# Part of the early loads and fills on ACT's queue, the first chunks also delivered turned, the first mixture's choices made for two or three chunks at a time, more tile buffers, and a new written-out order

## The reference, cut to what matters

```python
x = x + 0.5 * _L0_ffn_ref(_layernorm(x), ...)   # first mixture: 8 experts, 128 -> 512 -> 128, gelu
x = x + _L0_attn_ref(_layernorm(x), ...)        # conv, cumulative means of q and k, 128 -> 512 -> 128
x = x + 0.5 * _L0_ffn_ref(_layernorm(x), ...)   # first mixture again, same weights
x = x + 0.5 * _L1_ffn_ref(_layernorm(x), ...)   # second mixture: 16 experts, at most 320 tokens each
x = x + _L1_attn_ref(_layernorm(x), ...)        # a recurrence along each sequence
x = x + 0.5 * _L1_ffn_ref(_layernorm(x), ...)   # second mixture again

def _L0_ffn_ref(x, wr, br, w1, b1, w2, b2):     # of the 8 results only the chosen expert's is kept
    scores = einsum('bsh,he->bse', x, wr) + br
    expert_id = argmax(scores, axis=-1)
    h = gelu(einsum('bsh,ehf->ebsf', x, w1) + b1)
    y = einsum('ebsf,efh->ebsh', h, w2) + b2
    return einsum('ebsh,bse->bsh', y, one_hot(expert_id, 8))
```

## Time and profile before

| what | value |
|---|---|
| median of 3 runs | 824.54 us (823.46, 824.54, 829.46) |
| the profiled execution | 821.34 us, span 820.0 us |
| PE busy | 622.5 us, 76% |
| DVE busy | 444.1 us, 54% |
| POOL busy | 391.9 us, 48% |
| ACT busy | 336.5 us, 41% |
| mean granted clock of TensorE | 0.889 |
| moved by DMA | 94.87 MB, mean 116 GB/s |
| chain that ended last | PE 55%, issue 11%, DVE 10%, DMA 7%, POOL 6%, another core or an unknown queue 5% |

### The profile page before, as it was taken

How to read it: one execution, slowest core, us unless ns; L and a number is a source line. 1 busy time by engine, 2 the same in 40 slices (tenths; PEclk the granted TensorE clock), 3 DMA queues, 4 the chain that set the end, 5 groups by cost and what they waited for, 6 DMA issues and landing times.

```text
span 820.0 us, 13494 instructions
## 1 busy us (share of the span) xinstructions
PE 622.5 (76%) x3648; PEld 500.6 (61%) x3648; DVE 444.1 (54%) x1751; ACT 336.5 (41%) x993; POOL 391.9 (48%) x395
## 2 busy tenths in 40 slices
PE   6447588999988988996798742699965775397976
PEld 5437477978755755786688742476643664165654
DVE  5742145675889598563247633254436887043433
ACT  2113146646657535533347642343315543312411
POOL 1654535435421147245536667055464577234355
PEclk9998599999989999998899975699996975598998
DMA  8456278676200002344456323344533121233210
GB/s 323 142 188 202 86 214 257 173 217 217 79 1 0 1 21 94 96 128 134 121 163 195 99 70 145 82 140 117 155 97 103 56 68 63 73 104 98 62 31 13
DMA packets 74826, 94.87 MB, mean 116 GB/s; under 512 B 12610, under 2 KB 51305, under 8 KB 74496
## 3 DMA queue, kind: packets, MB, share of 16 engines
q1 hardware_dynamic: 64640, 79.46, 32.6%
q0 software_dynamic: 10112, 14.55, 5.3%
HBM read 65.71 MB, written 33.64 MB: 121 GB/s over the span
## 4 chain that ended last, share of the span: by engine, by line
PE 55%; issue 11%; DVE 10%; DMA 7%; POOL 6%; another core or an unknown queue 5%; ACT 3%; SPq 2%; DVEq 0%; ACTq 0%; POOLq 0%
PE ps L674 9%; PE ps L601 9%; PE ps L609 8%; PE ps L681 8%; POOL xs L1199 4%; PE ps L623 3%; PE ps L559 3%; PE ps L528 3%; PE ps L656 2%; PE ps L649 2%; DMA KC<-in_consts 2%; PE ps L664 2%; PE ps L592 2%; DMA xi<-xs 1%
## 5 line engine op out<-in xcount | busy, mean ns | idle before, releaser
L1108 ACT ACTIVATE ht<-ps,CL 128x128 f32<-128x128 f32 x368 | 103.8, 372 | 134.1 <-PE ps L601 77.9
L1199 POOL DMA_INDIRECT xs<-X,IDX x128 | 127.2, 994 | 63.1 <-issue 39.0
L1203 POOL DMA_INDIRECT y<-yt,xi x92 | 91.0, 989 | 124.2 <-DVE yt L909 104.5
L601 PE MATMUL ps<-xt,w1s 128*128 128x128 f32 x736 | 106.8, 295 | 24.6 <-DVE xt L903 12.6
L601 PEld LDWEIGHTS ps<-xt,w1s 128*128 128x128 f32 x736 | 97.0, 206 | 31.8 <-DVE xt L903 17.2
L609 PE MATMUL ps<-W,ht 128*128 x736 | 106.6, 296 | 10.4 <-issue 5.5
L609 PEld LDWEIGHTS ps<-W,ht 128*128 128x128 f32 x736 | 97.4, 208 | 16.6 <-issue 16.2
L1196 POOL TENSOR_TENSOR sma<-sma,MH 128x4 f32<-128x4 f32 (+1 forms) x40 | 48.4, 1215 | 64.5 <-DVE sma L719 53.4
L1165 ACT ACTIVATE hb<-ps 128x320 f32<-128x320 f32 x64 | 27.8, 437 | 108.0 <-PE ps L674 90.8
L1203 POOL DMA_INDIRECT y<-xu,x x36 | 34.3, 952 | 49.1 <-DVE xu L1017 33.9
L909 DVE SCALAR_TENSOR_TENSOR yt<-ps,xb 128x128 f32<-128x128 f32 x92 | 26.1, 287 | 58.0 <-PE ps L609 38.3
(11 more groups left out here) (153 smaller groups left out, 1241.0 us busy)
## 6 DMA issues: line engine op xcount, KB each, us to landing
w1s<-in_w SPq DMA_DIRECT2D x92, 256.0 KB
wx<-in_w1x SPq DMA_DIRECT2D x20, 512.0 KB
X<-y SPq DMA_DIRECT2D x24, 256.0 KB, 4.6
W<-in_w1x SPq DMA_DIRECT2D x12, 512.0 KB
xi<-xs SPq DMA_DIRECT2D x92, 66.0 KB
xs<-ZB SPq DMA_DIRECT2D x32, 165.0 KB
x<-xs SPq DMA_DIRECT2D x22, 132.0 KB
X<-in_x SPq DMA_DIRECT2D x8, 264.0 KB, 6.1
```

The costliest lines, as they stand in the source:

```text
L601: r = e.matmul(ps[TILE_BANKS[i % n]][:, c * P:(c + 1) * P], W1[i % NW1][:, c * P:(c + 1) * P], XTT[i % NX][:, :], start=True, stop=True)
L1108: r = e.activation(HT[i % NHT][:, c, :], ps[TILE_BANKS[i % len(TILE_BANKS)]][:, c * P:(c + 1) * P], ACT.Gelu, bias=CL[:, bass.ds(r0 * 4 + ...
L1199: return e.indirect_dma_start(dst, bass.IndirectOffsetOnAxis(ap=IDX[:, n:n + 1], axis=0), X[:, n, :], None, bounds_check=hi, oob_is_err=False)
L1203: return e.indirect_dma_start(dst, bass.IndirectOffsetOnAxis(ap=ix, axis=0), src, None, bounds_check=NT * P - 1, oob_is_err=False)
```

## The change

1. **Start.** The centring matrix and the router's weights come first, in one small load on SP's queue, then chunks 0 to 2, fill 0, chunks 3 to 7. ACT's queue carries the rest: chunks 0 and 1 of x already turned (`xt`, 256 KB each, made on the host, straight into the tile that pcopy fills), the first 8 numbers of the rows, the constants, W02, b2, CL, the second group's fill, the rows, MT and the rest of KC (stages bulk.0 to bulk.3, at the head of ACT's table), later the fills of groups 2 and 3 (bulk.4 and bulk.5, among its gelus).
2. **Turns.** `pturn` and `pcopy` are no longer done for chunks 0 and 1; their index is the chunk's less 2.
3. **Batches.** In the first mixture the epsilon (`peps`), `ppow`, `pnm`, `plog` and `oh` are done once for each batch of chunks: 0-1, 2-4, 5-7, and in the second pass 0-2, 3-4, 5-6, 7. The scores of a batch share one PSUM bank.
4. **Buffers.** NXI 8 to 16, NYT 4 to 12; `tload t` waits for home t-16, `ty t` for home t-12. Semaphores of loads still go round by 8 (a load waits for tn t-8), those of homes by 5. NW goes from 9 to 7.
5. `tup` no longer waits for the product of MT.
6. **Order.** All five tables are new.

```diff
-FILL_AFTER = [0, 0, 8, 12] + [18 + 3 * k for k in range(8)]
+TURNED = FIRST[0]
+
+BATCH = [range(0, 2), range(2, 5), range(5, 8), range(8, 11), range(11, 13), range(13, 15), range(15, 16)]
+BATCH += [range(k, k + 1) for k in range(2 * NC, 4 * NC)]
...
-        NXI, NXH, NX, NW1, NHT, NYT, NXB = 8, 3, 3, 4, 4, 4, 4
+        NXI, NXH, NX, NW1, NHT, NYT, NXB = 16, 3, 3, 4, 4, 12, 4
+
+        NXS, NHS = 8, 5
...
-        NW, NXE, NEN, NXET, NYTT, NYE = 9, 6, 2, 2, 2, 3
+        NW, NXE, NEN, NXET, NYTT, NYE = 7, 6, 2, 2, 2, 3
...
-            load_x(0)
-            e.dma_start(WR[:, :], wr).then_inc(sem("ck"), 16)
-            e.dma_start(KC[:, 0:K_INV], consts[:, 0:K_INV]).then_inc(sem("ck"), 16)
-            for c in range(1, FIRST[0]):
+            e.dma_start(KC[:, 0:K_ID], consts[:, 0:K_ID]).then_inc(sem("ca"), 16)
+            for c in range(TURNED + 1):
                 load_x(c)
-            e.dma_start(RW[:, 0:V_B2], rows[0:V_B2].partition_broadcast(P)).then_inc(sem("cb"), 16)
             SP.wait_ge(sem("zero"), 2)
             fill0(e, 0)
-            e.dma_start(CL[:, :], cols).then_inc(sem("cw"), 16)
-            for c in range(FIRST[0], NC):
+            for c in range(TURNED + 1, NC):
                 load_x(c)
-            e.dma_start(W02[:, :], w02).then_inc(sem("cw"), 16)
...
+                    if i >= NXS:
+                        SP.wait_ge(sem("tn"), i - NXS + 1)
                     if i >= NXI:
-                        SP.wait_ge(sem("tn"), i - NXI + 1)
-                        SP.wait_ge(sem(f"home{(i - NXI) % NYT}"), turns(i - NXI, NYT))
+                        wait_home(SP, i - NXI)
                         SP.wait_ge(sem("txb"), i - NXI + 1)
...
                     PE.wait_ge(sem(f"tw{i % NW1}"), turns(i, NW1))
-                    PE.wait_ge(sem("cenc"), 2)
...
-            ACTE.wait_ge(sem("ck"), 32)
-            e.activation(TRIM[:, :], KC[:, K_TRIM:K_TRIM + P], ACT.Copy).then_inc(sem("tri"), 1)
+            for c in range(TURNED):
+                e.dma_start(flat(XT[c]), xt[c * P:(c + 1) * P, :]).then_inc(sem("xt"), 16)
+            e.dma_start(RW[:, 0:E0], rows[0:E0].partition_broadcast(P)).then_inc(sem("cr"), 16)
+            e.dma_start(KC[:, K_ID:K_INV], consts[:, K_ID:K_INV]).then_inc(sem("ck"), 16)
             for stage, i in ORDER["act"]:
-                if stage == "cenc":
+                if stage == "bulk":
+                    if i == 0:
+                        e.dma_start(W02[:, :], w02).then_inc(sem("cw"), 16)
+                    elif i == 1:
+                        e.dma_start(RW[:, V_B2:V_END], rows[V_B2:V_END].partition_broadcast(P)).then_inc(sem("cw"), 16)
+                        e.dma_start(CL[:, :], cols).then_inc(sem("cw"), 16)
+                    elif i == 2:
+                        ACTE.wait_ge(sem("zero"), 2)
+                        fill0(e, 1)
+                    elif i == 3:
+                        e.dma_start(RW[:, E0:V_B2], rows[E0:V_B2].partition_broadcast(P)).then_inc(sem("cb"), 16)
+                        e.dma_start(MT[:, :], mats).then_inc(sem("cm"), 16)
+                        e.dma_start(KC[:, K_INV:K_END], consts[:, K_INV:K_END]).then_inc(sem("cm"), 16)
+                    else:
+                        ACTE.wait_ge(sem("tturn"), FILL_AFTER[i - 4])
+                        fill0(e, i - 2)
...
                 if stage == "ppow":
-                    POOL.wait_ge(sem("pstat"), 3 * (i + 1))
-                    power(extra(i % NC, R_R), SMP[i % NSM][:, 16:20]).then_inc(sem("ppow"), 1)
+                    n = len(BATCH[i]) * CT
+                    POOL.wait_ge(sem("peps"), i + 1)
+                    e.tensor_tensor(batch_x(i, R_R), SMP[i % NSM][:, 0:n], MH[:, 0:n], ALU.pow).then_inc(sem("ppow"), 1)
```

More of the change, by code:

```diff
@@ L49 @@
     [0, P, P, P, 4 * P, 4 * P, 4 * P, P, P, E1]).tolist()
[L52 removed]
+TURNED = FIRST[0]
+BATCH = [range(0, 2), range(2, 5), range(5, 8), range(8, 11), range(11, 13), range(13, 15), range(15, 16)]
+BATCH += [range(k, k + 1) for k in range(2 * NC, 4 * NC)]
+NB0 = sum(b[0] < 2 * NC for b in BATCH)
+BOF = {k: n for n, b in enumerate(BATCH) for k in b}
+BW = max(map(len, BATCH))
+FILL_AFTER = [8, 12] + [18 + 3 * k for k in range(8)]
 TABLE = {
     "sp": """
[L56 removed]
@@ new lines @@
+tdown.38 tturn.44 tdown.39 tup.41 tup.42 tturn.45 aq.0 tdown.40 tdown.41 tdown.42 tup.43 tup.44 tup.45 tdown.43 tdown.44 tdown.45 ak.0 av.0 aconv.1
+aturn3.0 aturn2.1 aturn1.2 aq.1 ak.1 aturn1.3 aconv.2 aturn4.0 av.1 aconv.3 aturn1.4 aturn3.1 aup.0 aturn2.2 aconv.4 ak.2 aq.2 aup.1 av.2 aturn2.3
+aup.2 aq.3 aturn3.2 aup.3 ak.3 aturn2.4 adown.0 aq.4 aturn4.1 av.3 aup.4 aup.5 aturn3.3 aup.6 aup.7 ak.4 aturn4.2 av.4 adown.1 aup.8 aup.9 aup.10
+aturn4.3 aup.11 aturn3.4 aup.12 adown.2 aup.13 aup.14 aup.15 aturn4.4 pturn.6 pturn.7 adown.3 aup.16 aup.17 aup.18 aup.19 pturn.8 pturn.9 adown.4
@@ new lines @@
+pscore.8 pscore.9 pturn.10 pscore.10 pscore.11 pscore.12 aturn1.5 aturn1.6 aturn1.7 aconv.5 rrank.2 aconv.6 rbase.2 aconv.7 aturn2.5 aq.5 ak.5 av.5
+aturn3.5 aturn2.6 aq.6 ak.6 aturn4.5 av.6 aup.20 aup.21 aup.22 aturn3.6 aup.23 aturn2.7 adown.5 aturn4.6 aq.7 aup.24 aup.25 aup.26 aup.27 ak.7 adown.6
+av.7 tturn.46 pturn.11 tup.46 tturn.47 aturn3.7 tup.47 tdown.46 pscore.13 tdown.47 pturn.12 tturn.48 tup.48 tturn.49 pscore.14 tup.49 tturn.50 aturn4.7
+tdown.48 tup.50 tdown.49 tturn.51 aup.28 tup.51 tdown.50 tturn.52 aup.29 aup.30 aup.31 tup.52 tturn.53 adown.7 tup.53 pturn.13 tturn.54 tdown.51
@@ L408, in wait_homes, with wait_home @@
         def wait_homes(lane, g):
-            for t in range(TILE0[g + 1] - NYT, TILE0[g + 1]):
-                lane.wait_ge(sem(f"home{t % NYT}"), turns(t, NYT))
+            for t in range(TILE0[g + 1] - NHS, TILE0[g + 1]):
+                wait_home(lane, t)
+        def wait_home(lane, t):
+            lane.wait_ge(sem(f"home{t % NHS}"), turns(t, NHS))
         def wait_scattered(lane, g):
@@ L885, in dve_program @@
                     xi, yt = XI[i % NXI], YT[i % NYT]
-                    DVE.wait_ge(sem(f"xi{i % NXI}"), turns(i, NXI))
+                    DVE.wait_ge(sem(f"xi{i % NXS}"), turns(i, NXS))
                     if i >= NXH:
@@ L907, in dve_program @@
                     if i >= NYT:
-                        DVE.wait_ge(sem(f"home{i % NYT}"), turns(i - NYT, NYT))
+                        wait_home(DVE, i - NYT)
                     e.scalar_tensor_tensor(out=YT[i % NYT][:, 0:P], in0=ps[TILE_BANKS[i % len(TILE_BANKS)]][:, 0:P], scalar=0.5,
@@ L1230, in pool_program @@
                     POOL.wait_ge(sem("ty"), i + 1)
+                    if i >= NHS:
+                        wait_home(POOL, i - NHS)
                     yt = YT[i % NYT]
-                    home(y[i >= TILE0[2]], yt[:, :], XI[i % NXI][:, R_ID:ROW].bitcast(U32)).then_inc(sem(f"home{i % NYT}"), 16)
+                    home(y[i >= TILE0[2]], yt[:, :], XI[i % NXI][:, R_ID:ROW].bitcast(U32)).then_inc(sem(f"home{i % NHS}"), 16)
                 elif stage == "apow1":
```

404 lines of the change are left out of this document (210 added, 194 removed).

## The result

The changed kernel took 841.68 us (median of 4 runs, 841.04 to 847.17), the kernel before beside it 824.25 (823.46 to 829.46). The ratio is 1.021, with a 95% interval of 1.015 to 1.027: slower, where I had forecast 811 and a gain. The profiled execution took 841.11 us, its span is 839.8.

The account below looks back on a forecast made before the run. PE was taken to bound 111 to 335 and 518 to 617 us, the start and tiles beside sends being loose. Terms -4.3 - 6 + 4 - 4 - 1 = -11.3 on 821.34 gave 810.0, plus 1: 811; range 792 to 829.

Parts of the forecast that it names:

- Start, first group: Up to the first send: scores of two chunks stand ahead of the base, first send near 22.7, 1.5 us later than 21.20.
- if both queues get equal shares: Loads at the start: 4.9 MB move in 15 us, so chunk 4 arrives just before PE wants it, costing nothing.
- third rival: Loads at the start: ACT's queue is served first, start and all behind it plus 8 us, 819 in all; chance 0.13.
- Start, second group: Up to the first tile product: row numbers at 43.6, no wait for fill or MT, product near 46.5, minus 4.3 us.
- signs of being wrong: Second group's sends after 47; holes over 30 or under 10 us; tile 15 to 46 over 232; ten table loads.
- First group's tiles: 50.8 to 111.3 us: hidden load and fewer buffer waits, holes of 18 to 20 us, minus 6 beside the start.
- first rival: Stretches with sends: unbroken indirect DMAs hold PE up in proportion, 0.77 us each, plus 14 and plus 5, 830; chance 0.12.
- Tile 15 to 46: 111 to 335 us: same work on a full PE, more attention stands alone, plus 4 us (bounds minus 3, plus 9).
- Second pass of the tiles: From 335 us: fewer table loads and larger buffers against new hole, minus 4; one send fewer behind the last norm, minus 1.
- 2.6 of new hole: 335 to 484 us: the third group's last 12 sends go in one run instead of a mix, plus 2.6 us.
- The rest: Second mixture: seven weight buffers leave six experts' lead, 37 us for a 512 KB load, cover enough, so no change.
- rival 2: Stretches with sends: holes hang on mixing sends and homes or on fills, and go; 794 in all; chance 0.25.

Follow-up runs that it names:

- d1: Kernel before with the second group's fill on SP's queue ahead of W02 and the first tile product not waiting for MT: 817.31 us beside 822.13, ratio 0.994.
- c1: The kernel before, unchanged, profiled again in another session where PE's signals come in time: 761.28 us.
- a2: Kernel before with 7 weight buffers instead of 9 in the second mixture, loads two experts back on SP's queue: 761.39 us beside 760.25, ratio 1.002.
- g1: Changed kernel with bulk loads behind ACT's first copies and the experts' first pass in the old order, signals late: 816.77 us beside before's 817.92, ratio 1.001.
- g2: Changed kernel with 1.05 us of POOL work behind each of the second group's 24 sends, NYT 11, signals late: 842.13 us beside before's 817.92.

## Why the prediction was wrong

- **Start, first group.** Forecast: ACT's issues done near 7.8 us (7.1 from 0.7), the router's weights ready near 8.4, first send 22.7. The issues were done at 13.3, the weights copied at 14.82, and the send went at 29.0: 6.4 us late at the weights, 6.3 at the send. The step that failed is the price of ACT's issues, 0.59 us each, taken from SP's loads before: the last three took 0.67, 2.29 and 4.52 us, and ACT's own copy stood behind them. The loads of x did land after 15.4 instead of 6.1 us, so "if both queues get equal shares, just before PE wants it" was wrong too, but it was not what the first send waited for. My third rival foresaw a loss by ACT's queue (+8), by another mechanism, late x; the first group did lose 7.8 us, and most of it was made up before the second group's sends.
- **Start, second group.** -4.3 forecast, -1.1 measured. The mechanism (no fill and no MT to wait for) was right: alone, in d1, it gave -3.9. The difference is the late row numbers, 46.8 instead of 43.6. In six of the eight traces with this start the first product went at 51.7 to 53.7, so there the start gained nothing at all (before 50.8 and, in c1, 51.6). One of my signs of being wrong came true too: the second group's sends started after 47, at 47.6.
- **First group's tiles.** Forecast -6 with "I take 18 to 20" us of holes; measured +4.6, with one wait of 29.33 us on the chain and 21.7 us without PE in the first 32.3. The step that failed is the assumption that half of PE's time is lost in a run, however long: PE had a third. On a timely machine, where there are no holes, the same stretch gave -6.7. The first rival had this mechanism, with 34 us of holes in all and 811 + 14 + 5 = 830. Its price per send was about right (24 x 0.77 = 18.5), but the homes behind the sends, which it counted too, came in no unbroken run: from 82.0 to 114.8 PE had 27.09 of 32.8 us.
- **Tile 15 to 46.** +4 forecast for attention that stands alone; -0.3 and -4.5 measured. The loss I feared from moving it behind more tiles did not come.
- **Second pass of the tiles.** -5 forecast, +4.7 measured. The ten table loads became eight beside the first, as forecast, yet on a timely machine the stretch gained only 0.2 us: what they and the larger buffers save wasn't on the path or was given back, which no run tells apart. The "2.6 of new hole" in the unbroken run of sends was too small: beside 14 DMAs in a row, 374 to 392 us, PE stood idle 4.55 and 11.15 us, where the forecast had 4.33 + 4.31 + 2.6 = 11.2 of holes. That the change loses in this stretch isn't shown (d1: 189.8 with the old order), only that the gain did not come.
- **"The rest": nothing.** Here the forecast lost most: +15.7 (9 to 18 over all pairs of late traces). It is true that seven buffers cost nothing (a2, on a timely machine), but I weighed only the buffers and not that PE's order of the experts was new too. It runs 20 up products in a row, the experts' results go home in runs of nine DMAs (544.5 to 555.5 and 604.5 to 615.5 us) where there had been none over six, and where signals are late that made holes of 11.2 us on the chain. The second pass had runs of nine both before and after, and its stretch differs by 15.0 and 9.5 us between the kinds. With the old order they were gone (g1: no wait of this kind on the chain from 519 to 616 us). I had named the danger, a dense run, and had not looked for it among the homes of the experts.
- **The range.** Its upper end was the first rival's value (830, written as 829; the lower, 792, stands for rival 2's 794). That rival was right in kind, and its price left out the experts' homes.

## What to carry to other kernels

When idle time in a profile has no recorded instruction at its end, find out what runs beside it and whether the same kernel shows it at all in another session, on another chip, before a change is priced on it: here 58 of 820 us were such time, and a change that gains 0.8% without it loses 2.1% with it. A new order must be read for every burst that it makes on a shared resource, also where its dependences look harmless. Bulk loads on a second queue are not free because the queue is: the engine that issues them was held up to 4.52 us by one issue, and its own work stood behind. Issue them behind the first work of that engine that others wait for.

## What I had not expected of the hardware

The same program took 818 to 824 us in three of the seven sessions and 760 to 764 in four, with the PE-bound stretch of the kernel before alike to 0.5 us. In the slower ones, DVE and ACT get PE's signals late (in the changed kernel's first run of sends 4.1, 14.7 and 8.7 us after the recorded end of the last product, by the trace's semaphore events) inside back-to-back runs of POOL's indirect DMAs (0.97 us each, 0.30 between), and not when one 1.05 us instruction of POOL stands between them (g2). Some signals come up to 2 us late also where no five such DMAs follow each other, as between 119 and 196 us of the changed kernel's trace. What makes a session of the one kind or of the other, and whether PE stands still or only its signals do, the traces don't tell; both stay open.
